# Attention's softmax sums: three key steps added on GpSimd, the fourth by an accumulating transfer out of a ring of five probability buffers

## What is computed

```python
qkv = (h @ Wqkv.T + bqkv).reshape(B, N, num_heads, hd, 3)
energy = jnp.einsum('bhqd,bhkd->bhqk', q, k)
att = jax.nn.softmax(energy, axis=-1) / D ** 0.5
out = jnp.einsum('bhqk,bhkd->bhqd', att, v)
out = out @ Wp.T + bp
```

## Time and profile before

| | us |
|---|---|
| median of 3 runs | 1870.91 (1868.19 to 1871.25) |
| the profiled execution, whole | 1865.17 |
| its span, first to last instruction | 1863.0 |
| PE busy in the span | 1811.2 (97%) |
| POOL busy in the span | 1218.1 (65%) |
| pairs 0 to 120 of attention, product with v to product with v | 793.5 |

### The profile page before, as it was taken

The page is one execution under the profiler, slowest core; times in us unless marked ns, Lnnn a source line. Parts: engine busy times, 40 slices in busy tenths (PEclk is TensorE's granted clock), DMA queues, the critical chain, the costliest instruction groups (busy, mean ns, idle before and its releaser), DMA issues. The chain is left out here.

```text
span 1863.0 us, 27079 instructions
## 1 busy us (share of the span) xinstructions
PE 1811.2 (97%) x9510; PEld 1211.8 (65%) x9510; DVE 1257.2 (67%) x1986; ACT 835.1 (45%) x1545; POOL 1218.1 (65%) x679
## 2 busy tenths in 40 slices
PE   8989999999999999999999999999999999999996
PEld 4678888888888788888555545554555555554485
DVE  4655655655655575566877777777778777777289
ACT  3223123122223122122366666666666666666465
POOL 2675465465464243332488888888988898898565
PEclk9999999999999999999999999999999999999898
DMA  7410110110103657595877787777777787865796
GB/s 272 117 35 23 57 34 23 56 34 23 56 1 115 213 191 248 192 274 188 199 165 176 180 180 179 177 183 180 178 182 182 177 185 171 186 152 134 237 385 226
DMA packets 135373, 287.10 MB, mean 154 GB/s; under 512 B 23984, under 2 KB 41520, under 8 KB 127200
## 3 DMA queue, kind: packets, MB, share of 16 engines
q1 hardware_dynamic: 102996, 200.10, 35.5%
q0 software_dynamic: 9264, 66.11, 17.5%
q10 hardware_dynamic: 23008, 19.54, 3.3%
HBM read 134.68 MB, written 84.19 MB: 117 GB/s over the span
## 5 line engine op out<-in xcount | busy, mean ns | idle before, releaser
L1618 DVE TENSOR_REDUCE at_mrow<-banks 128x1 f32<-128x512 f32 x976 | 594.2, 681 | 163.0 <-PE banks L1464 162.7
L1714 POOL TENSOR_TENSOR at_sums<-at_probs 128x2048 f32<-128x2048 f32 x127 | 597.2, 4702 | 89.1 <-DMA at_sums<-at_sums 78.5
L1598 ACT ACTIVATE at_probs<-banks 128x512 f32<-128x512 f32 x1024 | 519.0, 624 | 179.4 <-PE banks L1482 174.1
L1464 PE MATMUL banks<-early_ks,early_qs 96*128 96x512 f32 x976 | 407.0, 417 | 9.4 <-DVE at_mrow L1618 5.4
L1482 PE MATMUL banks<-early_qs,early_ks 98*128 98x512 f32 x1024 | 408.5, 418 | 1.8 <-ACT at_probs L1598 1.8
L1464 PEld LDWEIGHTS banks<-early_ks,early_qs 96*128 96x128 f32 x976 | 184.8, 189 | 141.1 <-DVE at_mrow L1618 87.9
L1482 PEld LDWEIGHTS banks<-early_qs,early_ks 98*128 98x128 f32 x1024 | 193.8, 190 | 107.3 <-ACT at_probs L1598 83.8
L1494 PE MATMUL banks<-at_probs,at_v 128*32 128x512 f32 x2048 | 251.5, 609 | 0.0
L66 PE MATMUL banks<-l_nt,l_weights 128*128 128x512 f32 x768 | 180.7, 396 | 5.4 <-DVEq L1193 4.3
L66 PE MATMUL banks<-l_ht,l_weights 128*128 128x512 f32 x768 | 177.5, 390 | 1.9 <-issue 1.9
L657 ACT ACTIVATE l_gt<-banks,mod 128x512 f32<-128x512 f32 x60 | 45.1, 777 | 298.9 <-PE banks L526 262.7
(11 more groups left out here) (147 smaller groups left out, 2157.8 us busy)
## 6 DMA issues: line engine op xcount, KB each, us to landing
at_sums<-at_sums POOLq DMA_DIRECT2D x63, 1024.0 KB, 8.2
qk_scratch<-qk_out SPq DMA_DIRECT2D x64, 512.0 KB, 6.1
early_ks<-qk_scratch SPq DMA_DIRECT2D x48, 512.0 KB, 4.9
early_qs<-qk_scratch SPq DMA_DIRECT2D x96, 256.0 KB, 5.6
attn_scratch<-at_out SPq DMA_DIRECT2D x32, 512.0 KB, 7.3
o_a<-attn_scratch SPq DMA_DIRECT2D x32, 512.0 KB, 12.5
chunk_in<-x SPq DMA_DIRECT2D x8, 1024.0 KB, 5.4
v_scratch<-qk_v ACTq DMA_DIRECT2D x32, 256.0 KB, 2.9
```

Of the source, the lines that this page charges most:

```text
L1464: pe.matmul(em[n % 3][:], qs[0:96, slot, half, j, c * P:(c + 1) * P], ks[0:96, slot, j, keys * CH:(keys + 1) * CH], start=True, stop=True) ...
L1598: nc.scalar.activation(probs[:, i % 4, j, :], et[n % 3][:], ACT.Exp).then_inc(exp_done, 1)
L1618: nc.vector.tensor_reduce(mrow[:, half, keys, u:u + 1], em[n % 3][:], AX.X, ALU.max).then_inc(max_done, 1)
L1714: nc.gpsimd.tensor_tensor(into, probs[:, a], probs[:, a + 1], ALU.add).then_inc(pair_ready, 1)
```

## The change

The first add of a quad stays. The second add now adds the third step alone onto the same tile, and the accumulating transfer reads the fourth step's probabilities where ACT wrote them. `sums` loses its third tile and `probs` gains a fifth, so the memory used is the same.

```diff
+        PROBS_RING = 5
...
-        probs = sb("at_probs", [P, 4, HG, CH])
-        sums = sb("at_sums", [P, 3, HG, CH])
+        probs = sb("at_probs", [P, PROBS_RING, HG, CH])
+        sums = sb("at_sums", [P, 2, HG, CH])
...
+        def slot_of(g, i):
+
+            return (STEPS * g + i) % PROBS_RING
+
...
-                    if not (first and i < 4):
-
-                        act.wait_ge(av_done, STEPS * g + i - 3)
-                        act.wait_ge(pair_ready, PAIRS * g + (i - 4) // 2 + 1)
+                    if not (first and i < PROBS_RING):
+
+                        old = STEPS * g + i - PROBS_RING
+                        act.wait_ge(av_done, old + 1)
+                        if old % 4 == 3:
+                            act.wait_ge(quad_ready, 16 * (old // 4 + 1))
+                        else:
+                            act.wait_ge(pair_ready, 2 * (old // 4) + (1 if old % 4 < 2 else 2))
...
-                    pool.wait_ge(exp_done, HG * (STEPS * g + 2 * pair + 2))
-                    if second and quad >= 1:
-
-                        pool.wait_ge(quad_ready, 16 * quad)
-                    if not second and quad >= 2:
-
-                        pool.wait_ge(den_done, quad - 1)
-                    into, a = sums[:, 2 if second else quad % 2], 2 * pair % 4
-                    nc.gpsimd.tensor_tensor(into, probs[:, a], probs[:, a + 1], ALU.add).then_inc(pair_ready, 1)
-                    if second:
+                    total = sums[:, quad % 2]
+                    i = 2 * pair
+                    if not second:
+
+                        pool.wait_ge(exp_done, HG * (STEPS * g + i + 2))
+                        if quad >= 2:
+
+                            pool.wait_ge(den_done, quad - 1)
+                        nc.gpsimd.tensor_tensor(total, probs[:, slot_of(g, i)], probs[:, slot_of(g, i + 1)], ALU.add).then_inc(pair_ready, 1)
+                    else:
+
+                        pool.wait_ge(exp_done, HG * (STEPS * g + i + 1))
+                        pool.wait_ge(pair_ready, PAIRS * g + pair)
+                        nc.gpsimd.tensor_tensor(total, total, probs[:, slot_of(g, i)], ALU.add).then_inc(pair_ready, 1)
+                        pool.wait_ge(exp_done, HG * (STEPS * g + i + 2))
                         pool.wait_ge(pair_ready, PAIRS * g + pair + 1)
-                        pool.dma_start(sums[:, quad % 2].rearrange("p j c -> p (j c)"), into.rearrange("p j c -> p (j c)"),
+                        if quad >= 1:
+
+                            pool.wait_ge(quad_ready, 16 * quad)
+                        pool.dma_start(total.rearrange("p j c -> p (j c)"), probs[:, slot_of(g, i + 1)].rearrange("p j c -> p (j c)"),
                                        accum_op=ALU.add).then_inc(quad_ready, 16)
```

More of the change, by code:

```diff
@@ L1493, in av @@
                     rows = slice(HD * j, HD * (j + 1))
-                    last = pe.matmul(av_ps[rows, :], v[:, slot, kc, rows], probs[:, kc % 4, j, :],
+                    last = pe.matmul(av_ps[rows, :], v[:, slot, kc, rows], probs[:, slot_of(g, i), j, :],
                                      start=kc == 0, stop=kc == KC - 1)
@@ L1556, in _ @@
             pe.wait_ge(pair_ready, PAIRS * G - 1)
-            tiles = [sums[:, (QUADS * G - 1) % 2], probs[:, 2], probs[:, 3]]
+            tiles = [sums[:, (QUADS * G - 1) % 2]] + [probs[:, slot_of(G, i)] for i in (-2, -1)]
             for tile in tiles:
@@ L1597, in group @@
                         act.wait_ge(et_done, n + 1)
-                        nc.scalar.activation(probs[:, i % 4, j, :], et[n % 3][:], ACT.Exp).then_inc(exp_done, 1)
+                        nc.scalar.activation(probs[:, slot_of(g, i), j, :], et[n % 3][:], ACT.Exp).then_inc(exp_done, 1)
                     if g == 1 and i % KC in (3, 5):
```

## The result

| | before | after |
|---|---|---|
| median, us | 1869.36 (1868.19 to 1871.25, 5 runs) | 1889.82 (1878.01 to 1890.71, 5 runs) |
| ratio, 95% interval | | 1.0083 (1.0067 to 1.0099) |
| profiled execution; span | 1865.17; 1863.0 | 1878.01; 1875.9 |
| pairs 0 to 120 | 793.5 | 806.7 |

The forecast was 1856.9, in 1850 to 1868, with 6% for slower. On another chip the changed kernel came to 1876.95 (1871.36 to 1883.62, 6 runs), ratio 1.0047. (The ratio is not that of the two medians, which in the table are 1.1% apart.) Its runs lie 12 us apart each time; those of the kernel before lie 3 us apart in the five above and 8.5 in the 21 on the other chip. The profiled execution is the fastest of its five, so its trace explains 12.9 us and not the 20.5 between the medians.

The account below looks back on a forecast made before the run. PE's program was taken as the floor, with 18.3 us lost above it to POOL's add-transfer-landing loop. Regaining 4.3, 9.0, 0.5 and 0.7 less 0.5 gives 14.0 us: 1870.9 to 1856.9, range 1850 to 1868.

Parts of the forecast that it names:

- The floor, 25.87 us for four pairs: PE's own program in attention, with its three banks; a quad takes 12.94 us and the change doesn't touch it.
- POOL's waits for the landing go; what is late next is POOL's own order: POOL's second add: its 76.7 us of waits vanish; multiply, round_off and remain around the adds then set the issue.
- Issue at a + 10.4 for odd quads, 11.6 for even: Accumulating transfer's issue after the quad's first product with v; gains 1.4 to 2.4 us odd, 0.6 even.
- The adds at 4.6 us, no price for in-place: POOL's 128x2048 adds: same count, one now in place, bounded between 4.55 and 4.9 us, taken at 4.6.
- ACT's new wait ends last nowhere: ACT's wait for a landing at steps 0, 4, 8, 12 of a group costs nothing, as PE already waited.
- The transfer at 8.2 us: The 1 MB accumulating transfer, now read from a probability tile, taken at 8.2 us, between 8.2 and 9.1.
- Rival B: Traffic sets the landing, so an earlier issue only lengthens the transfer; 0 to 3 us gained, 1869; chance 0.12.
- (b), 9.0 of 10.7 us back: DVE's reciprocal waits for the denominators' spread, PE lacks a bank at pairs 3 and 7; 9.0 of 10.7 us regained.
- (a), 4.3 of 4.8 us back: PE stands before a denominator until the quad's transfer lands; 4.3 of 4.8 us regained.
- Rival C: Slower: even quads' transfer outgrows its 9.2 us and PE loses the excess at 30 even quads; 1877; chance 0.06.
- All three losses hang on one loop: Late denominators, reciprocals and negated maxima blamed on POOL's add, transfer and landing: 13.4 to 13.7 us against 12.94.

Follow-up runs that it names:

- hold6: Changed kernel, with odd quads' accumulating transfer held until the sixth exponential of the next pair; 1886.22 us, ratio 1.0093.
- after_ef: Changed kernel with SyncE's 512 KB loads of parts 1 and 3 moved ahead of the reciprocals' broadcast; 1858.11 us, 0.9953; again 1854.60 us, 0.9952.
- before_ef: Kernel before, with only the 512 KB loads of parts 1 and 3 moved ahead of the wait for the reciprocals' store; 1861.21 us, 0.9943; again 0.9972.
- late2: Changed kernel with multiply and round_off behind the even quad's transfer, reciprocal one pair later, 512 KB loads ahead of the reciprocals' store; 1856.76 us, 0.9943.
- late: Changed kernel with multiply and round_off moved from ahead of the adds to behind the even quad's transfer; 1872.05 us, ratio 1.0019.
- mult_first: Changed kernel with multiply in front of the odd quad's transfer instead of behind it; 1901.53 us, ratio 1.0159.

## Why the prediction was wrong, step by step

The prediction took 14.0 us off the profiled execution; 12.9 came on top. Of these 27 us, the late denominators are 14.6 (4.3 less forecast, 10.3 more measured), the longer fronts 10.3, the late negated maxima 2.1. Two steps failed: the even quads' issue, for which `multiply`'s wait for the broadcast was put at next to nothing, and the transfer's 8.2 us.

- *The floor, 25.87 us for four pairs.* Right (25.86 after).
- *POOL's waits for the landing go; what is late next is POOL's own order.* The first half is right. The second is the first step that failed. Behind the waits came a DMA, the broadcast, which in the kernel before had 3.4 us to itself in the mean because the transfer was late. The prediction says only that `multiply` often waits a little, and doesn't name the broadcast among what the earlier transfer could meet. In the kernel before, `multiply`'s wait had 0.8 us in the list, and the broadcast had landed about when the odd transfer went out, 0.1 to 1.7 us ahead of `multiply`: a margin against the very transfer that the change moves. In the changed kernel that wait was 53.6 us.
- *Issue at a + 10.4 for odd quads, 11.6 for even.* Right: 10.45, and 11.05 even, where the broadcast was not caught.
- *The adds at 4.6 us, no price for in-place.* Right: 4583 ns mean for the in-place add, 4619 for the other.
- *ACT's new wait ends last nowhere.* Right: its list has one wait of 0.5 us for an add and none for a landing.
- *The transfer at 8.2 us.* Wrong: 8.9 by the median, 9.07 for odd quads (7.70 before). The landing came 0.8 us sooner, not 1.7 to 2.4. This is the second step that failed. Rival B named it and I gave it 0.12; `hold6` to `after` show its size, 0.4 us of landing for 1 us of issue, and `after_ef` its cause.
- *(b), 9.0 of 10.7 us back.* The path was right, the size was not. At its own places, pairs 3 and 7 of a group, about 7 us are left, so near 4 came back, and the reciprocal's wait fell from 16.4 to 10.3; the spread follows the odd landing by 8.3 to 8.7 us, and where the landing was at 5.03 (`after_ef`) the wait is 1.2. All fronts together are 12.2 us too long in place of 10.9, for some 5 us of slower clock behind the stalls (below).
- *(a), 4.3 of 4.8 us back.* Wrong in sign: 10.3 us more, 11.1 of it in even quads. Rival C has the place and the sign (even quads) but its mechanism carries only 1.5 us of the 13.7, in four quads whose transfer took 10.4 us or more. The other 12.2 are five quads whose issue slipped, by up to 6.6 us.
- *All three losses hang on one loop.* Wrong, and before any collision. That a loop is 13.4 to 13.7 us long where it waits says only that it waits; that is 4 to 6% over 12.94, where the prediction counts it as some 2%. `before_ef` leaves the loop its waits, 60.3 us, and gains 0.3 to 0.6%; taking the loop away as well (`after_ef`) gains 0.2% more or nothing. Only in the order of `late2` do the old adds cost 0.6%. The reciprocals' losses hung on when the landing was, and that on what shared the DMA engines with the transfer.

## What to carry to other kernels

Before a transfer is issued sooner, list what other queues issue in the 3 us ahead of its new place and who stands behind each of those in an in-order queue; a wait near zero there can be a margin, not slack. When the DMA engines are full at that point, an earlier issue buys a fraction of itself (here 0.4), and moving a load that nobody needs soon may buy more than the reordering: here 0.3 to 0.6% for a few lines, in either kernel. And a chain of waits that is longer than the bound proves nothing until it is taken away with all else in place.

## What the hardware showed that was not expected

A small transfer can take as long as a large one that is issued near it. Four loads of 64 KB, median 2.0 us to landing each, had landed 9.7 us after the first was issued, with the 1 MB transfer 0.7 us behind them. The 8 KB spread took at most 7.6 us in all traces of this case but four times, when the accumulating transfer was issued 0.02 to 0.8 us ahead of it: then it took 9.3 (`late`, above), 9.6 (`late2`), 9.7 and 11.2 us (`mult_first`). Two spreads with that transfer 0.3 to 0.4 us behind them took 1.9 and 5.0.

A stall of PE costs more than itself. After the 3.21 us of idling at 1412 to 1416 the granted clock fell to 0.54 of full speed, the 1.2 GHz level for most of the 8 us after it (stretches: busy us of each engine, PE clock, share of DMA engines, GB/s):

```profile
1408.00:1412.00 4.00, 4.00 (x26) 1.65 (x24) 3.56 (x6) 3.03 (x7) 3.77 (x3) 1.00 0.65 131
1412.00:1416.00 4.00, 0.79 (x16) 0.42 (x16) 0.00 (x0) 0.60 (x1) 3.86 (x2) 1.00 0.98 262
1416.00:1420.00 4.00, 3.33 (x19) 2.25 (x8) 1.67 (x3) 1.19 (x2) 3.56 (x1) 0.54 0.19 58
1420.00:1424.00 4.00, 4.00 (x15) 2.88 (x17) 3.04 (x5) 3.16 (x6) 2.17 (x2) 0.60 1.05 239
1424.00:1428.00 4.00, 4.00 (x26) 1.99 (x18) 2.53 (x5) 1.76 (x5) 3.65 (x1) 1.00 0.81 168
```

The front of that pair took 6.64 us where a clean one takes 4.13: 2.5 us on top of 3.4.
